# Attention and expert layer on one core: the expert tables read eight entries at a time

## What is computed

```python
def _L0_ffn_ref(x, router_w, w1, b1, w2, b2):
    xf = x.reshape(-1, D)
    logits = jnp.einsum('td,ed->te', xf, router_w)
    top_vals, top_idx = jax.lax.top_k(logits, K)          # K = 2 of E = 8
    probs = jax.nn.softmax(top_vals, axis=-1)
    out = jnp.zeros_like(xf)
    for e in range(E):
        w = jnp.sum(jnp.where(top_idx == e, probs, 0.0), axis=-1)
        h = jax.nn.gelu(jnp.einsum('td,fd->tf', xf, w1[e]) + b1[e], approximate=False)
        y = jnp.einsum('tf,df->td', h, w2[e]) + b2[e]
        out = out + w[:, None] * y
    return out.reshape(orig_shape)
x = x + _L0_xattn_ref(_layernorm(x), ctx_1024, ...)       # 16 heads of 8
x = x + _L0_ffn_ref(_layernorm(x), ...)
```

## Time and profile before

| | us |
|---|---|
| median of 3 runs | 479.35 |
| the three runs | 482.87, 478.46, 479.35 |
| span of the profiled execution | 482.4 |
| the profiled execution's own time, by its span the first of the three runs | 482.87 |
| TensorE busy, whole span | 345.6 |
| the expert loop on TensorE, first to last matmul | 294.1 to 457.5 |

### The profile page before, as it was taken

One profiled execution on the slowest core, in us unless ns is written; L12 is line 12 of the kernel. 1 busy time (PEld: TensorE's weight loads), 2 busy tenths in 40 slices (PEclk: granted clock), 3 DMA queues, 4 the chain that ended last, 5 costly groups with the idle time before them and its releaser, 6 DMA issues.

```text
span 482.4 us, 12377 instructions
## 1 busy us (share of the span) xinstructions
PE 345.6 (72%) x3715; PEld 272.1 (56%) x3715; DVE 282.5 (59%) x883; ACT 228.3 (47%) x536; POOL 223.8 (46%) x316
## 2 busy tenths in 40 slices
PE   2527798897887978674872006998999899988800
PEld 0214466565656555452652005998898889788800
DVE  7258799979688978494455641444444444344426
ACT  1313587857474846365451002665555555545500
POOL 7775233414155534345367730555554455545510
PEclk9956899989796978798675555999999999999965
DMA  4696445544352342011001225565656565566268
GB/s 126 160 236 193 107 120 109 145 133 125 97 151 76 107 114 58 24 53 39 25 30 40 66 65 151 169 173 166 186 168 173 162 181 171 163 174 180 84 194 329
DMA packets 57119, 63.00 MB, mean 131 GB/s; under 512 B 14109, under 2 KB 40116, under 8 KB 56896
## 3 DMA queue, kind: packets, MB, share of 16 engines
q1 hardware_dynamic: 51584, 53.22, 40.6%
q0 software_dynamic: 4320, 8.47, 5.1%
q10 hardware_dynamic: 1152, 0.53, 0.4%
HBM read 37.65 MB, written 11.88 MB: 103 GB/s over the span
## 4 chain that ended last, share of the span: by engine, by line
PE 37%; DVE 24%; SPq 15%; issue 11%; DMA 6%; ACT 3%; POOL 2%; another core or an unknown queue 1%; ACTq 0%; POOLq 0%; DVEq 0%
DVE shift L1209 9%; PE smax L1140 8%; PE sexp L1149 7%; PE smax L929 6%; PE tail L973 4%; DMA stacks<-dispatch_d 3%; SPq L496 3%; SPq L488 3%; SPq L495 3%; PE feed L920 3%; SPq L489 2%; PE feed L1008 2%; SPq L411 2%; DVE xs L1601 2%; POOL dispatch_d L636 2%
## 5 line engine op out<-in xcount | busy, mean ns | idle before, releaser
L1209 DVE TENSOR_REDUCE shift<-smax 128x4 f32<-128x512 f32 x128 | 85.6, 683 | 37.1 <-PE smax L929 36.0
L775 ACT ACTIVATE probs<-sexp 128x512 f32<-128x512 f32 x128 | 74.0, 593 | 38.5 <-PE sexp L937 31.5
L704 POOL DMA_INDIRECT result_d<-y_out,stacks x71 | 70.5, 992 | 38.5 <-issue 38.5
L636 POOL DMA_INDIRECT dispatch_d<-rows_out,row_i x64 | 62.6, 978 | 54.3 <-DVE shift L1209 27.5
L1580 DVE TENSOR_TENSOR probs<-smax,b_cols 128x512 f32<-128x512 f32 x71 | 49.1, 692 | 64.7 <-PE smax L1140 52.5
L1140 PE MATMUL smax<-probs,w_ring 128*128 128x128 f32 x568 | 80.4, 286 | 3.8 <-ACT probs L880 1.7
L1149 PE MATMUL sexp<-w_sb,probs 128*128 x568 | 77.6, 280 | 0.7 <-ACT probs L884 0.7
L1140 PEld LDWEIGHTS smax<-probs,w_ring 128*128 128x128 f32 x568 | 70.7, 195 | 10.1 <-issue 8.2
L929 PE MATMUL smax<-stacks 64*128 64x128 bf16 x512 | 53.9, 235 | 30.8 <-DVE shift L1209 17.0
L1149 PEld LDWEIGHTS sexp<-w_sb,probs 128*128 128x128 f32 x568 | 69.7, 193 | 2.1 <-issue 1.1
L929 PEld LDWEIGHTS smax<-stacks 64*128 64x128 bf16 x512 | 31.5, 101 | 59.1 <-DVE shift L1209 32.8
(11 more groups left out here) (191 smaller groups left out, 521.7 us busy)
## 6 DMA issues: line engine op xcount, KB each, us to landing
w_ring<-w_t_dram SPq DMA_DIRECT2D x71, 256.0 KB
stacks<-kpart SPq DMA_DIRECT2D x48, 128.0 KB
stacks<-qpart SPq DMA_DIRECT2D x48, 128.0 KB
stacks<-dispatch_d SPq DMA_DIRECT2D x71, 65.0 KB
stacks<-result_d SPq DMA_DIRECT2D x16, 256.0 KB, 6.1
ctx<-ctx_t_dram SPq DMA_DIRECT2D x8, 256.0 KB, 3.0
w_sb<-w_t_dram SPq DMA_DIRECT2D x8, 256.0 KB
out_dram<-xs SPq DMA_DIRECT2D x8, 256.0 KB, 4.8
```

The source lines that it names most:

```text
L636: nc.gpsimd.indirect_dma_start(out=dispatch_d, out_offset=bass.IndirectOffsetOnAxis(ap=row_i[r % RR][:, k, b:b + 1], axis=0), in_=rows_out ...
L704: nc.gpsimd.indirect_dma_start(out=result_d, out_offset=bass.IndirectOffsetOnAxis(ap=xg[r][:, D + 1:D + 2].bitcast(U32), axis=0), in_=y_ou ...
L775: nc.scalar.activation(dst, sexp[hp][:], ACT.Exp).then_inc(exp_done, 1)
L1209: nc.vector.tensor_reduce(shift4[n % 2][:, hp, 0, 4 * m:4 * m + 4], smax[hp][:], AX.X, ALU.max, negate=True).then_inc(max_taken, 1)
```

## The change

`BULK` = 8. A new helper reads up to eight neighbouring entries of a table with one load instruction and gives eight register values, each with the same bounds as before. SyncE, TensorE and VectorE use it at the start and then at every tile whose number is a multiple of eight; in between the tiles take their value from the eight registers. On SyncE both tables are read that way, ahead of `load_w1` of that tile; on TensorE after `down(t - 1)`, ahead of `up(t + 1)`; on VectorE ahead of `add_bias(t)`. At the start SyncE reads eight experts ahead of the first w1 transfer and eight starts ahead of the waits for the scattered rows. TensorE reads eight after the first transpose.

```diff
+BULK = 8
...
+        def table_values(engine, row, t, high):
+
+            return nc.values_load_multi_w_load_instructions(row[0:1, t:min(t + BULK, TILES)], engines=(engine,),
+                                                            min_val=0, max_val=high)[1]
...
-            def load_tile(t, r, reuse):
-                if reuse:
+            def load_tile(t, r, at):
+                if t >= TRING:
                     sp.wait_ge(y_sent[r], ring_count(t - TRING, r))
-                at = sp.value_load(start_of[0:1, t:t + 1], min_val=0, max_val=EXPERTS * REGION)
                 sp.dma_start(xg[r], dispatch_d[bass.ds(at, P), :]).then_inc(xg_loaded[r], 16)
 
-            def load_w1(t, r):
+            def load_w1(t, r, e):
...
-                e = sp.value_load(expert_of[0:1, t:t + 1], min_val=0, max_val=EXPERTS - 1)
...
+            experts = table_values(mybir.EngineType.SP, expert_of, 0, EXPERTS - 1)
             for t in range(AHEAD):
-                load_w1(t, t)
+                load_w1(t, t, experts[t])
+            starts = table_values(mybir.EngineType.SP, start_of, 0, EXPERTS * REGION)
             for r in range(ROUND - RR, ROUND):
                 rows_gone(sp, r)
...
             for t in range(AHEAD, TILES):
-                load_w1(t, t % WRING)
-                load_tile(t, t % TRING, t >= TRING)
+                if t % BULK == 0:
+                    experts = table_values(mybir.EngineType.SP, expert_of, t, EXPERTS - 1)
+                    starts = table_values(mybir.EngineType.SP, start_of, t, EXPERTS * REGION)
+                load_w1(t, t % WRING, experts[t % BULK])
+                load_tile(t, t % TRING, starts[t % BULK])
...
-            before_e, e, next_e = None, expert_reg(0), expert_reg(1)
+            experts = table_values(mybir.EngineType.PE, expert_of, 0, EXPERTS - 1)
             for t in range(TILES):
                 up(t, t % 2)
                 if t + 1 < TILES:
                     turn_tile(t + 1, (t + 1) % 2, (t + 1) % TRING)
                 if t:
-                    down(t - 1, (t - 1) % 2, before_e)
-                before_e, e, next_e = e, next_e, (expert_reg(t + 2) if t + 2 < TILES else None)
-            down(TILES - 1, (TILES - 1) % 2, before_e)
+                    down(t - 1, (t - 1) % 2, experts[(t - 1) % BULK])
+                if t and t % BULK == 0:
+                    experts = table_values(mybir.EngineType.PE, expert_of, t, EXPERTS - 1)
+            down(TILES - 1, (TILES - 1) % 2, experts[(TILES - 1) % BULK])
...
-            before_e, e = None, expert_reg(0)
+            experts = table_values(mybir.EngineType.DVE, expert_of, 0, EXPERTS - 1)
             for t in range(TILES):
-                add_bias(t, t % 2, e)
+                before_e = experts[(t - 1) % BULK]
+                if t and t % BULK == 0:
+                    experts = table_values(mybir.EngineType.DVE, expert_of, t, EXPERTS - 1)
+                add_bias(t, t % 2, experts[t % BULK])
                 if t:
                     sum_y(t - 1, (t - 1) % 2, before_e)
-                before_e, e = e, (expert_reg(t + 1) if t + 1 < TILES else None)
-            sum_y(TILES - 1, (TILES - 1) % 2, before_e)
+            sum_y(TILES - 1, (TILES - 1) % 2, experts[(TILES - 1) % BULK])
```

More of the change, by code:

```diff
@@ L504, in _ @@
             for t in range(AHEAD):
-                load_tile(t, t, False)
+                load_tile(t, t, starts[t])
             for t in range(AHEAD, TILES):
-                load_w1(t, t % WRING)
-                load_tile(t, t % TRING, t >= TRING)
+                if t % BULK == 0:
[3 more added lines that the diff above has]
+                load_tile(t, t % TRING, starts[t % BULK])
             for r in range(TRING):
@@ L1152, in down @@
                 last.then_inc(down_done, 1)
-            def expert_reg(t):
-                return pe.value_load(expert_of[0:1, t:t + 1], min_val=0, max_val=EXPERTS - 1)
             pe.wait_ge(table_steps, TABLE_STEPS)
@@ L1569, in _ @@
             assert table[0] == TABLE_STEPS, table[0]
-            def expert_reg(t):
-                return dve.value_load(expert_of[0:1, t:t + 1], min_val=0, max_val=EXPERTS - 1)
             def add_bias(t, i, e):
```

## The result

The changed kernel takes 493.49 us in the median of 4 runs (490.27 to 496.38), against 479.5 (478.46 to 482.87): ratio 1.0287, 95% interval 1.0222 to 1.0352.

What follows compares the result with a forecast made beforehand. SyncE's queue, not the matmuls, was taken to often set the expert loop's pace. Start +7.1, TensorE's loop +0.3 and SyncE late +3.2 sum to +10.6 us, forecast 490 from the median 479.35, range 469 to 508.

Steps and rivals of the forecast that it cites:

- What bounds the kernel: Expert loop: SyncE hands out tiles at 2.29 us each, while TensorE needs 2.04 unstarved, with a floor of 1.90.
- my three signs of being wrong: Forecast wrong if checks shrink, TensorE's hole is under 2 us, or iterations between lumps stay at 2.04 or above.
- The lump: checks stay, only the load is saved: Every eight tiles, one load, then eight checks and asserts in a row; 3.3 us on SyncE, which has two.
- rival 3: Register checks: load cheap and each check 0.05, since 0.15 holds a wait for data; -10, 469 us; chance 0.13.
- x: Cost of one more register inside a grouped load: taken as 0.12 us, between ends of 0 and 0.27.
- rival 2: Grouped load: eight entries cost what one does, x below 0.05; 477 us; chance 0.25.
- rival 1: Grouped load: eight registers load one after another at nearly full price; 504 us, or 516 at 0.27; chance 0.22.
- Start: From the table to the first product: SyncE's two lumps and TensorE's load of eight (+2.2) delay it, +7.1 us.
- The loop on TensorE: Tile 3 to 70: 127.3 bare plus eight lumps of 3.0 exposed, 151.3 against 151.0: +0.3 us.
- VectorE at nothing: Ahead of the bias addition: VectorE's lump delays bias 2.9 us but hides behind TensorE's lump, costing nothing.
- The 2.9 x 8 = 23: VectorE's lump in the loop: up to 23 us if TensorE's own lump did not cover it.
- SyncE just late at every eighth tile, +3.2: SyncE's dispatch transfer lands at 11.5 where TensorE wants it at 11.4; 0.4 taken for each of eight, +3.2 us.

Runs made afterwards that it cites:

- the load of eight that begins at entry 2: Against the kernel before: eight entries per load on SyncE alone, tiles 0 and 1 read singly, first grouped load behind their transfers; 472.48 us, ratio 0.9832.
- Without the checks: The changed kernel with the bounds checks of the eight values left out: 458.41 us, ratio 0.9545 against the kernel before; again 462.3, ratio 0.96.
- the group of four: Later profiles on one chip: kernel before 464.24 us, changed kernel 472.25, four entries per load 459.52, SyncE alone with two 456.81 and eight 454.11.

## Why the prediction was right, and where it was not

**What bounds the kernel.** Right. SyncE was the pace and TensorE's floor is 1.90 us a tile. Relieving SyncE alone gave a loop of 137.6, where 67 x 2.04 makes 136.7; removing the checks gave 129.4, where the bare loop was put at 127.3. Iterations between lumps are 1.90, as said. None of my three signs of being wrong came: the checks did not shrink, the holes are over 2 us, and the iterations between lumps stay under 2.04.

**The lump: checks stay, only the load is saved.** Right, and it decides the sign. The other reading (rival 3, the 0.15 is a wait for the loaded number) falls: in the lump, seven checks follow a load that is long back, and they take 146 to 147 ns as before.

**The price of one more register.** Wrong size. I took x = 0.12; measured are 0.037 on SyncE ((527 - 268) / 7), 0.043 on VectorE, 0.054 on TensorE. By that alone rival 2 was the case. With x = 0.04 on SyncE and 0.05 on TensorE the same steps add up to +2, 481; neither that nor rival 2's 477 is what was measured. The rule of the Trainium skill ("Runtime: NRT & Kernel Launch", "Instruction fetch mechanics", some 200 ns a register even in bulk) is not borne out for the loads of the changed kernel: four registers cost 31 ns more than one, eight 259 more. It is borne out for the load of eight that begins at entry 2: (1675 - 268) / 7 makes 0.201 us a register. So the dear load of rival 1 exists, and the changed kernel escaped it because its loads begin at multiples of eight.

**Start.** Put at +7.1, measured +4.7. With the measured x the same steps give 2 x (2.46 + 0.26) + 1.38 = 6.8 to the tile's transfer; it was 6.6. On TensorE they give +1.8, and it was +1.7 (landing to first product 3.53 against 1.80). Nearly all of the error is x; the remaining 0.5 us is the transfer of the first rows, which landed after 1.69 instead of 2.17 us.

**The loop on TensorE.** 3.0 exposed per lump was put down, 2.4 to 2.7 measured; again x (0.14 + 7 x 0.29 + 7 x 0.05 = 2.5). The step that failed is a missing one: the holes are also followed by iterations at half clock, 1.7 us each time, after three of eight lumps in both profiles of the changed kernel. That is 5 us a loop, and I had the granted clock at 1.00 in every stretch of before and no term for it. 127 + 8 x 2.5 + 5.1 = 152; measured 154.8 and 152.8. In the first of these, two more places, at tiles 54 and 57, take 1 us too long each. The one at tile 54 is in other kernels' profiles too (see "Without the checks"), the one at tile 57 is not explained.

**VectorE at nothing.** Right: with the lump on TensorE alone the holes are as long as in the changed kernel. Without that cover it does have a price: with VectorE's lump alone, TensorE waits eight times up to 1.6 us, 11.8 in all. The 2.9 x 8 = 23 was an upper bound.

**SyncE just late at every eighth tile, +3.2.** Wrong: no such wait is there. With the measured x the two lumps are 5.4 instead of 6.6, and the tile's rows leave 1.2 us sooner than in my count, which is more than the 0.1 by which they were late.

So the terms were 7.1 + 0.3 + 3.2 = 10.6, and what was measured behind the table is 4.7 + 3.8 - 0.5 = 8.0. The dear register load that I assumed made the sum about 9 us too large; the half clock that I left out (5.1) and the two slow places (2.1) made up for most of that. That the total was close is luck. More luck is in the 14.0 us of the first comparison: the spans of the two profiles differ by 11.9, of which 3.8 stand ahead of the table, in code that the change does not touch. Whether anything of it belongs to the change is not settled; with 267.4 against 267.7, 268.1 and 274.0 in the group of four, nothing speaks for it, and in that group the whole difference was 6.7 to 8.0.

**Two slips in the working.** I took the profiled execution before to be the run of 482.87, with 0.5 us around its span. In every later run the time is 2.0 to 2.2 us above the span, so it took about 484.5, an estimate from these, and is none of the three. The forecast is not touched, since it was made from the median. And in rival 3, 8 x 0.7 is 5.6 and not 5.9.

**That long holes bring the half clock, and short ones don't,** is shown only as far as this: 3 and 3 of 8 holes of 2.5 us, 4 of 8 with the lump on TensorE alone, 1 of 8 at the 1.6 us holes of VectorE's lump, 0 of 34 holes of 1.0 us. In the kernel before TensorE has waits of up to 1.5 us in the loop, with the granted clock at 1.00 throughout. Reading four at a time changes the distance between the holes together with their length, so which of the two matters is open, and what decides among the eight was not tried.

## What to carry to other kernels

Grouping saves only the part that is per instruction. List what is per value (here the bounds check and assert, 0.27 us, of which nothing went), for what stays per value comes as one lump, and a sequencer that hid most of 0.7 us per iteration behind queued matmuls does not hide 3 us once in eight. Ask engine by engine: the same edit gave -9 us (by the medians) on the queue that was the bound and had six tiles of lead, and cost time on the two engines that run in step with the matmuls. If entries are read in groups, begin each group at a multiple of four entries and make its length one too: the two loads here that began elsewhere took three times as long. Before grouping, see whether the checks are needed at all: the tables here are bounded by how they are computed, and leaving the checks out, with one entry per load, gave a loop of 129.4 (ratio 0.9522), where the best grouping that kept them gave 135.9 (ratio 0.9719).

## What the runs showed of the hardware

- A load of consecutive entries into registers costs on SyncE 268 ns for one, 476 for two, 680 for the three at the end of the table when read by four, 299 for four, 527 for eight, and 925 to 1009 for the seven at the end when read by eight. These fit one step of about 0.2 us for each group of four and for each single entry left over; that this is how the load works is my reading of the durations. I had expected the cost to rise evenly with the number of registers.
- The groups of four count only where the load begins right: all loads of four and eight above begin at a multiple of four. The two loads of eight that begin at entry 2 took 1675 and 1667 ns, as much as eight single steps (268 + 7 x 201 = 1675).
- The two comparisons and the logical step of a check take 146 to 152 ns on SyncE and TensorE and 183 to 190 on VectorE, wherever they stand; address products and sums in the same instruction form take 42 to 57.
- Holes of 2.5 us in an otherwise full TensorE are followed at times by a granted clock of 0.5 for about two tiles; holes of 1.0 us never were.
